# One of five sender one-hots of each attribute batch is fetched from a table by GpSimd

## What is computed

```python
h = relu(layernorm(x))                       # layer 0: three rounds of mean aggregation
for i in range(3):
    tmp = tmp + segment_sum(tmp[src], dst) / max(deg, 1)
    res = res + tmp / (1 + i)
x = x + res
h = relu(layernorm(x))                       # layer 1: a node MLP with edge means
rec_attr  = scatter_mean(edge_attr_16, dst)  # edge_index[1] in the program's layout
sent_attr = scatter_mean(edge_attr_16, src)  # mean of the edges that a node sends
x = x + mlp(concat([h, rec_attr, sent_attr]))
```

## Time and profile before

| what | value |
|---|---|
| median of three runs | 2169.39 us (2167.29 to 2172.15) |
| the profiled execution | 2168.65 us |
| its span, first to last instruction | 2166.8 us |
| busy over the span | DVE 82%, PE 75%, PEld 59%, ACT 51%, POOL 40% |
| visit loop (one-hots of the adjacency) | about 64 to 298 us |
| steps with attribute batches | about 330 to 803 us |
| mean granted TensorE clock | 0.837 over the span, 1.00 in most of the steps with batches |

### The profile page before, as it was taken

How to read it: one execution, slowest core, us unless ns; L and a number is a source line. 1 busy time by engine, 2 the same in 40 slices (tenths; PEclk the granted TensorE clock), 3 DMA queues, 4 the chain that set the end, 5 groups by cost and what they waited for, 6 DMA issues and landing times.

```text
span 2166.8 us, 36534 instructions
## 1 busy us (share of the span) xinstructions
PE 1626.5 (75%) x8603; PEld 1278.6 (59%) x8603; DVE 1787.4 (82%) x5315; ACT 1101.3 (51%) x2852; POOL 863.5 (40%) x861
## 2 busy tenths in 40 slices
PE   3666668988998989454777778677467888887876
PEld 2322247877887876333666667676355555665555
DVE  8999988999998996886787787886677778778776
ACT  1777757777886964010424334335444444444443
POOL 2000000000000000277777777771047777777771
PEclk9887779999999998675879788798668777778888
DMA  6465567656665762446656656663022222222221
GB/s 211 147 183 163 172 198 277 246 192 243 243 244 198 256 253 82 123 126 167 182 161 169 173 165 178 171 170 92 24 65 55 54 55 54 55 54 55 55 56 45
DMA packets 192503, 314.87 MB, mean 145 GB/s; under 512 B 25906, under 2 KB 139449, under 8 KB 182451
## 3 DMA queue, kind: packets, MB, share of 16 engines
q1 hardware_dynamic: 163344, 248.12, 35.2%
q0 software_dynamic: 27712, 63.56, 11.3%
q10 hardware_dynamic: 1250, 0.86, 0.2%
HBM read 232.38 MB, written 80.07 MB: 144 GB/s over the span
## 4 chain that ended last, share of the span: by engine, by line
POOL 32%; issue 12%; DVE 11%; PE 10%; DMA 3%; ACT 1%; DVEq 0%; POOLq 0%; ACTq 0%
POOL G L699 18%; POOL G L687 8%; POOL SCR L687 5%; PE PS L1926 3%; PE PS L1927 2%; DVE HOT_R L1183 2%; PE PS L1902 1%; DMA G<-table,src_idx 1%; PE PS L1817 1%; DVE GROUPED_R L1198 1%; DVE GROUPED_R L1192 1%; ACT HB L721 1%; PE PS L1703 1%; PE PS L1878 0%; DMA gathered_rows<-G 0%
## 5 line engine op out<-in xcount | busy, mean ns | idle before, releaser
L687 POOL DMA_INDIRECT G<-table,src_idx x252 | 268.3, 1065 | 932.2 <-DMA table<-RX 853.1
L699 POOL DMA_INDIRECT G<-table,src_idx x415 | 408.4, 984 | 248.8 <-issue 125.6
L2033 PE MATMUL PS<-SCR,OH 128*128 128x256 f32 x830 | 286.5, 511 | 102.4 <-DVE SCR L1656 102.2
L2033 PEld LDWEIGHTS PS<-SCR,OH 128*128 128x128 f32 x830 | 204.9, 256 | 156.4 <-DVE SCR L1656 114.8
L1817 PE MATMUL PS<-ALL_R 128*128 128x256 f32 (+3 forms) x2025 | 266.0, 288 | 24.9 <-DVE ALL_R L1246 9.1
L1902 PE MATMUL PS<-RX,OH 128*128 x830 | 175.3, 366 | 138.2 <-DVE SCR L1358 86.5
L1817 PEld LDWEIGHTS PS<-ALL_R 128*128 128x128 f32 (+1 forms) x2025 | 251.1, 190 | 27.8 <-issue 11.0
L1902 PEld LDWEIGHTS PS<-RX,OH 128*128 128x128 f32 x830 | 145.9, 240 | 169.1 <-issue 163.9
L1926 PE MATMUL PS<-AT 128*128 128x128 f32 x830 | 203.9, 332 | 20.2 <-issue 11.4
L1777 PE MATMUL PS<-HOT_R,GROUPED_R 128*119 128x448 f32 x830 | 191.2, 377 | 24.5 <-DVE G L1204 22.9
L892 ACT COPY SCR<-PS 128x640 f32<-128x640 f32 x83 | 57.4, 692 | 290.2 <-PE PS L2008 290.2
(11 more groups left out here) (400 smaller groups left out, 3327.2 us busy)
## 6 DMA issues: line engine op xcount, KB each, us to landing
ALL_R<-adjacency SPq DMA_DIRECT2D x72, 1600.0 KB, 6.8
adjacency<-ALL_R SPq DMA_DIRECT2D x26, 1600.0 KB, 7.3
AT<-gathered_rows SPq DMA_DIRECT2D x103, 256.0 KB, 3.9
gathered_rows<-G SPq DMA_DIRECT2D x63, 256.0 KB, 2.4
AT<-dst_in_block SPq DMA_DIRECT2D x103, 128.0 KB, 4.1
G<-table,src_idx POOLq DMA_INDIRECT x667, 2.5
gathered_rows<-SCR SPq DMA_DIRECT2D x40, 256.0 KB, 2.2
table<-RX SPq DMA_DIRECT2D x10, 320.0 KB, 2.7
```

The source lines that it names most:

```text
L687: pool.indirect_dma_start(score_rows(i)[:, q], None, tables[0], bass.IndirectOffsetOnAxis(ap=src_idx[:, v:v + 1], axis=0)).then_inc(s(f"sc ...
L699: pool.indirect_dma_start(G[:, p, q, :], None, tables[i], bass.IndirectOffsetOnAxis(ap=src_idx[:, VB * k + q:VB * k + q + 1], axis=0)).the ...
L2033: ins = pe.matmul(PS[:, q, 0:MSG], OH[:, p, q, :], view(SCR, M_AT + (p * VB + q) * MSG, [[1, MSG]]), start=True, stop=True)
```

## The change

One of the one-hots that DVE makes, that of visit 3, is no longer computed. Its rows are fetched by an indirect DMA from a table `group_table` of 512 x 448 numbers in DRAM, whose row r has a one at place r (1 to 448). POOL builds the table once: after `idx_made` four compares of 128 x 448 (one for 128 rows) into `SCR` at `HIGH0_AT`, and one DMA of 917 KB (512 x 448 x 4 bytes) to DRAM. DVE adds one cast that turns the places of the visits 3 into whole numbers to serve as indices, and waits for the store of the table ahead of its work behind the visit loop. Then POOL runs through the 83 batches: it waits until batch k-2 is summed and issues one gather of 128 rows of 1792 bytes (229 KB). PE waits for that gather ahead of the matmuls of the batch. The semaphores of the score stage's gathers are shared and renamed, with their counts moved.

```diff
+        group_table = dram("group_table", [4 * P, NSRC])
...
+            for i in range(2):
+                pool.wait_ge(s(f"radial_rows_stored{i}"), 32)
+            for c in range(4):
+                pool.tensor_scalar(view(SCR, HIGH0_AT + c * NSRC, [[1, NSRC]]), iota_h[:, 0:NSRC], bv[:, c:c + 1], None, ALU.is_equal).then_inc(s("groups_made"), 1)
+            pool.wait_ge(s("groups_made"), 4)
+            pool.dma_start(group_table.rearrange("(c p) n -> p c n", p=P), view(SCR, HIGH0_AT, [[NSRC, 4], [1, NSRC]])).then_inc(s("groups_stored"), 16)
+            pool.wait_ge(s("groups_stored"), 16)
+            for r in range(RING):
+                pool.wait_ge(s(f"block_moved{r}"), 16 * stored(r))
+            pool.wait_ge(s("block_summed"), FIRST)
+            for k in range(NB):
+                if k >= 2:
+                    pool.wait_ge(s("attrs_summed"), k - 1)
+                at = view(EI, 2 * VW + VB * k + 3, [[1, 1]]).bitcast(I32)
+                pool.indirect_dma_start(hot_src(k % 2, 3).bitcast(F32), None, group_table, bass.IndirectOffsetOnAxis(ap=at, axis=0)).then_inc(s(f"rows_gathered{k % 2}"), 16)
...
             dve.wait_ge(s("fill_copied_act"), N_FILL)
+            dve.tensor_copy(view(EI, 2 * VW + 3, [[VB, NB]]).bitcast(I32), view(EI, 2 * VW + 3, [[VB, NB]]))
             dve.tensor_copy(src_idx[:], EI[:, 0, 0:NV + 1]).then_inc(s("idx_made"), 1)
...
             dve.wait_ge(s("normed_act"), ACT_GROUPS)
+            dve.wait_ge(s("groups_stored"), 16)
...
-                for q in (2, 3):
-                    src_hot_of(q)
+                src_hot_of(2)
                 dve.wait_ge(s("dve_step"), left_made)
                 dve.tensor_copy(part16(2), left).then_inc(s("attrs_hot"), 1)
...
                 pe.wait_ge(s("dst_hot"), 2 * k + 2)
+                pe.wait_ge(s(f"rows_gathered{k % 2}"), 16 * (k // 2 + 1))
                 for q in range(VB):
                     for j in range(PARTS_L):
                         pe.matmul(PS[0:LA, 2, 0:NSRC], grouped(p, j)[:, q * LA:(q + 1) * LA], hot_src(p, q),
```

More of the change, by code:

```diff
@@ L355, in fill_copy @@
             return dst, view(PS, fill_bank(f) * 512, [[P, n], [1, w]])
+        hot_fetches = lambda i: len(range(i, NB, 2)) if i < 2 else 0
         def hot_src(p, q):
@@ L615, in _ @@
                             slot, w = n % ROWS_RING, SIZE[n] * D
-                            sp.wait_ge(s(f"score_gathered{slot}"), 16 * SB * (n // ROWS_RING) + 16 * SIZE[n])
+                            sp.wait_ge(s(f"rows_gathered{slot}"), 16 * hot_fetches(slot) + 16 * SB * (n // ROWS_RING) + 16 * SIZE[n])
                             sp.dma_start(gathered_rows[:, n * SB * D:n * SB * D + w], score_rows(slot).rearrange("p a b -> p (a b)")[:, 0:w]).then_inc(s(f"rows_stored{slot}"), 16)
@@ L687, in _ @@
                     pool.indirect_dma_start(score_rows(i)[:, q], None, tables[0],
-                                            bass.IndirectOffsetOnAxis(ap=src_idx[:, v:v + 1], axis=0)).then_inc(s(f"score_gathered{i}"), 16)
+                                            bass.IndirectOffsetOnAxis(ap=src_idx[:, v:v + 1], axis=0)).then_inc(s(f"rows_gathered{i}"), 16)
             pool.wait_ge(s("species_loaded"), 32)
@@ L1353, in rate @@
                     i, n = k % ROWS_RING, SIZE[k]
-                    dve.wait_ge(s(f"score_gathered{i}"), 16 * SB * (k // ROWS_RING) + 16 * n)
+                    dve.wait_ge(s(f"rows_gathered{i}"), 16 * hot_fetches(i) + 16 * SB * (k // ROWS_RING) + 16 * n)
                     dve.wait_ge(s("z_made"), k + 1)
```

## The result

The changed kernel takes 2151.95 us in the median of four runs (2148.17 to 2154.26); the kernel before took 2169.24 beside it. The ratio is 0.9924 with a 95% interval of 0.9902 to 0.9945: 17.3 us less, where 21.6 less had been forecast. The profiled execution is the fastest of the four, 2148.17 us with a span of 2146.4.

What follows compares the result with a forecast made beforehand. DVE was taken to set the pace, PE following closely. Terms -27.6 + 1.7 + 1 + 3.3 = -21.6 us from the profiled 2168.65 gave 2147.0, stated as 2147.5 us (-1.0%), range 2140 to 2157.

Steps and rivals of the forecast that it cites:

- Part 1: DVE's batches: one one-hot less saves 0.365 us each from batch 2 on, nearly all reaching the end: -27.6 us.
- Part 2: Beside DVE's visit loop: POOL's four table compares cost 1.5 us and DVE's cast 0.15; +1.7 us (0 to 2.5).
- Part 3: PE's wait for the gather: landing in 5.0 us is covered, narrowly only at the 14 double steps; +1 us.
- Part 4: DVE's batches: POOL's gathers slow DVE instructions by 0.04 us a batch; +3.3 us, between nothing and 16.6.
- DVE stays the slowest, by 0.6 us of 30.7: Second round, six batches on five steps after the change: DVE takes 30.7 us, PE 30.1, ACT 28.5.
- the 2 us taken off: Deducted from the one-hot's 29.6 us gain, for the thin margin to PE and PE's own third-round pace.
- So 5.0 us is covered: Gather landing including POOL's wake-up against PE's window: tightest 5.4 us in double steps, over 9 with one batch a step.
- four turns of 0.42 us: On each DMA engine, four gather packets each let one of SP's packets pass, adding 1.7 us to the landing.
- three signs of being wrong: PE waiting for the gather's DMA over a few us, one-hot instruction beyond 473 ns, DVE waiting for ACT or PE every batch.
- second rival: The gather comes late for 28 batches in and behind double steps; landing at 7.1 us costs 31 us, 2178; chance 0.09.
- point of decision at 6.8 us: Gather landing, the time of SP's own fetch, from which lateness of about 22 us decides against the change.
- third rival: Gathers stop DVE for most of POOL's 0.947 us instruction; half of it costs 39 us, 2183; chance 0.05.

Runs made afterwards that it cites:

- no gather: The changed kernel without table, gathers and their waits, DVE making visit 3's one-hot for batches 0 and 1 only: 2139.25 us, ratio 0.9881.
- both: The changed kernel with three buffers for the fetched one-hot instead of two, and the table built before the visit loop: 2138.22 us, ratio 0.9867.
- experiment 8: The changed kernel with gathers landing in unread memory, without SP's adjacency fetches, POOL not waiting for batches: gathers land in 3.3 us; no total time given.
- experiment 2: The changed kernel with all gathers landing one after the other in memory no batch reads, PE not waiting for them: 2172.24 us, ratio 1.0027.
- experiment 9: The kernel before plus table and 83 gathers landing in memory no batch reads, DVE still making all four one-hots: 2163.45 us in one run.
- early table: The changed kernel with POOL building and storing the table earlier, before DVE's visit loop: 2148.19 us, ratio 0.9903.

## Why the prediction was right, and where it was wrong

The time, 2152, lies within the forecast's own range, and the sign and the mechanism hold. The terms:

| step | forecast | measured | from |
|---|---|---|---|
| Part 1, a one-hot less | -27.6 | -25.2 | no gather against before, batches |
| Part 2, table | +1.7 | +2.3 | visit loop 235.5 against 233.2 |
| Part 3, gather and its wait | +1 | +8.1 | after against no gather, batches |
| Part 4, POOL beside DVE | +3.3 | 0.0 | both against no gather, batches |
| sum | -21.6 | -14.8 | |

So the terms are 7 us off in all, and by luck no more: Part 4, put at 3.3, cost nothing, and that hides nearly half of the 7.1 by which Part 3 was put too low. The traces' own shift of the last batch is 13.4 us; the 1.4 us between are the loop's start, the first dense steps and the first fetch, each up to 0.6 later. The medians give 17.3 with an interval of some 12 to 21, which holds both; what the medians show above them can't be told from the scatter behind the last batch.

**What bounds the kernel.** DVE did set the pace before, as the earlier trace rows said: taking 0.365 us a batch off it gave 25 of 29.6 us. Of the 2.4 us that the measured 25.2 lacks to the forecast's 27.6, 1 is the clock at the first round change, 0.70 without gathers where the kernel before had 1.00 (the batch behind it comes 6.25 us later instead of 5.20). "DVE stays the slowest, by 0.6 us of 30.7" failed in two of three rounds. The 5.56 us for PE's step had been read early in the first round; in the second PE needs 5.37 to 5.44, and DVE after the change 5.77 - 0.365 = 5.41: a tie, where single steps give their whole 0.36. In the third round PE's 5.47 is reached, 0.23 below the 5.70 of before, and that is the 2 us taken off and some more.

**Part 3 was mis-sized, and it is the step that failed.** "So 5.0 us is covered" rested on a landing of 4.7: 3.0 for a gather alone, and 1.7 for the fetches beside it. The first term held: alone the gather takes 3.3 (experiment 8). The second did not: the fetches add 2.7 us beside the changed kernel's steps (6.0 in the median, experiment 2), so the landing is past the tightest window of 5.4; beside the steps of the kernel before, whose rows the forecast had, it is 5.0 (experiment 9). Nor do the runs bear out four turns of 0.42 us: about 0.9 of the 2.7 pass before the gather's first packet starts, twice the one turn that the sum had there, and with half of the packets 2.3 were added still. What the rest consists of stays open. That the gather has 64 packets came out right by luck: "two rows" was read from a mean of 3.15 KB, and the packets are of three rows, two rows and 4 bytes. The window itself had been named rightly: the 13 late gathers are all for the second batch of a double step or the one behind it.

Two of the three signs of being wrong that the prediction gave itself came: PE waits 15.2 us for the gather's DMA in L1797, and L1203 reaches 611 ns. The first marks the step that failed, and the forecast's range of up to 2157 had room for it; the second cost nothing (Part 4 below). The third, DVE waiting for ACT or PE in every batch, did not come (7 waits for PE of 10.0 us, 11 for ACT of 6.5 us, in 83 batches).

**The second rival's price was too high** in turn. For a landing of 7.1 it charged 28 batches 1.1 us each, 31 us. 13 of them were late, 17.7 us in all, and the loss at the end was 8.1, because DVE and ACT run ahead while PE stands. A point of decision at 6.8 us doesn't exist in that form: with gathers that PE met 5.4 to 7.7 us after their issue the kernel still gained 17.

**Part 2** lies at its upper bound, but not for the reason given. The nearest row (0.52 us for POOL's iota) had the instruction's size wrong. Ahead of the loop, where DVE does other work, the early table's four compares take nearly as long as beside it:

```profile
4.80 5.75 POOL L668 TENSOR_SCALAR SCR<-iota_h,bv 128x448 f32<-128x448 int16 x4 [1.02 <-DVE bv L1007]
```

That is 1.4 us for one. So 2.1 us for all four was no bound on how long they run: they run for 6.03 us beside the loop, and DVE loses 2.3 to 2.6 of these, not all. With the early table the loop takes 233.2 us again, though it begins later. **Part 4** was nothing: the steps are 5.85 us in the first round with and without gathers. L1203 has a longest instruction of 611 ns (473 before), but its median stays 447:

```profile
L1203 DVE TENSOR_SCALAR HOT_R<-iota_h,EI x249: 430/447/611, 333.3 to 783.6; 128x448 fp32r<-128x448 int16 x125
L696 POOL DMA_INDIRECT HOT_R<-group_table,EI x83: 944/977/1699, 333.6 to 779.9; - x83
```

So the third rival is out. The Trainium skill's rule of a lock between GpSimd and DVE ("SBUF — State Buffer", Who interferes with whom) agrees with the compares, beside which DVE's instructions take up to 0.62 us instead of 0.25. Whether it is also behind single longer gathers (1.70 us, median 0.98) isn't shown; no step became longer by them. SP's fetches land in 7.6 us instead of 6.8; PE waits for none of them from 345 us on, as forecast.

## What to carry to other kernels

A transfer that replaces an engine's work needs its landing measured beside the traffic it will meet: alone it took 3.3 us, beside the stream of fetches 6.0, and the lead of two buffers was 5.4 at its tightest. One more buffer took all waits for the gather away; a quarter of the row would have left 5.8 us of them. And a wait counts nearly in full only where its engine is the bound: of 4.6 us of waits in the DVE-bound round 0.1 was lost, and of 5.5 in the PE-bound one 4.6.

## What the runs showed that was not expected

The granted clock behind a stop of PE is not the same from kernel to kernel: behind the same wait of 3.0 us it was 1.00 in the kernel before and 0.68 in the kernel of experiment 9, which cost 1.3 to 1.5 us each time. In the changed kernel it was down behind two of the waits for the gather as well (0.77 and 0.76). What decides it these runs don't show. Part of what looks like contention in a stage's sum can be this; it is told apart by the length of the ten matmuls (3.01 against 2.27 us).
